# Graph-attention logits in a fused two-layer kernel: first layer through diagonal fp32 matmuls, squares on ScalarE, third layer partly on TensorE, softmax moved into the gather stage

## The reference

```python
sph = jnp.stack([rho, theta, phi], axis=-1)
feat = jnp.concatenate([sph, sph - jnp.mean(sph, axis=-1, keepdims=True)], axis=-1)
h = lrelu(_bn(feat @ W1.T, g1, b1))      # 6 planes
h = lrelu(_bn(h @ W2.T, g2, b2))         # 3 planes
h = lrelu(_bn(h @ W3.T, g3, b3))         # 1 plane
att = jax.nn.softmax(h[..., 0], axis=-1)
agg = jnp.einsum('bnkc,bnk->bnc', xk, att)
return x + agg.transpose(0, 2, 1)
```

## Time and profile before

| | us |
|---|---|
| median of 3 runs | 6926.59 |
| lowest and highest run | 6912.48, 6935.65 |
| the profiled execution: its time, its span | 6927.13, 6925.3 |
| from the start to the logit block | 5136.4 |
| logit block | 526.3 |
| gather stage | 1262.6 |

### The profile page before, as it was taken

One profiled execution on the slowest core, in us unless ns is written; L12 is line 12 of the kernel. 1 busy time (PEld: TensorE's weight loads), 2 busy tenths in 40 slices (PEclk: granted clock), 3 DMA queues, 4 the chain that ended last, 5 costly groups with the idle time before them and its releaser, 6 DMA issues. The chain is left out here.

```text
span 6925.3 us, 166962 instructions
## 1 busy us (share of the span) xinstructions
PE 4994.0 (72%) x63824; PEld 2889.3 (42%) x63824; DVE 5517.1 (80%) x7158; ACT 3973.8 (57%) x8974; POOL 2391.2 (35%) x3108
## 2 busy tenths in 40 slices
PE   6887887878778787878878778884000029999999
PEld 3444444444444444444444444442000017676676
DVE  8877777878778777877877878873779988888887
ACT  4666655666566566665655556665322237777776
POOL 2444444444444444544544444443000001111111
PEclk8878878887887887887887787885555559999999
DMA  1000000000000000000000000000000000000000
GB/s 37 13 14 14 14 14 26 14 14 14 14 14 26 14 14 14 14 14 26 14 14 14 14 14 26 14 7 4 0 0 0 0 7 33 29 30 29 32 29 27
DMA packets 35795, 114.00 MB, mean 16 GB/s; under 512 B 5488, under 2 KB 6128, under 8 KB 34800
## 3 DMA queue, kind: packets, MB, share of 16 engines
q1 hardware_dynamic: 34928, 102.28, 4.2%
HBM read 68.71 MB, written 33.55 MB: 15 GB/s over the span
## 5 line engine op out<-in xcount | busy, mean ns | idle before, releaser
L550 ACT ACTIVATE ohT<-oh_ps,cst 128x512 bf16<-128x512 f32 x1920 | 1277.1, 691 | 388.1 <-PE oh_ps L430 383.3
L448 PE MATMUL g_ps<-tparts,ohT 128*128 128x24 bf16 x23040 | 921.5, 178 | 797.6 <-ACT ohT L550 787.7
L448 PEld LDWEIGHTS g_ps<-tparts,ohT 128*128 128x128 bf16 x23040 | 765.3, 100 | 1438.2 <-ACT ohT L550 1336.0
L794 DVE MAX8 vals<-pd_sb 128x8 f32<-128x1024 f32 x1024 | 1205.3, 1213 | 133.2 <-ACT pd_sb L550 112.5
L799 DVE FIND_INDEX8 idx<-vals,pd_sb 128x8 uint16<-128x1024 f32 x1024 | 1244.2, 1218 | 0.0
L801 DVE MATCH_REPLACE8 pd_sb<-vals,pd_sb 128x1024 f32<-128x1024 f32 x768 | 927.7, 1208 | 0.0
L430 PE MATMUL oh_ps<-bitsT,code 128*128 128x512 bf16 x1920 | 872.7, 460 | 2.2 <-ACT bitsT L707 2.2
L550 ACT ACTIVATE pd_sb<-pd_ps,nxx 128x512 f32<-128x512 f32 x512 | 355.1, 694 | 864.9 <-PE pd_ps L354 864.2
L1684 PEld LDWEIGHTS e_a_ps<-planes,e_oh 120*128 120x128 bf16 x24576 | 688.1, 97 | 244.1 <-issue 179.1
L818 DVE TENSOR_REDUCE mx<-s_ps 128x8 f32<-128x512 f32 x256 | 176.5, 689 | 721.1 <-PE s_ps L389 721.1
L1500 ACT COPY e_at<-e_a_ps 128x512 f32<-128x512 f32 x512 | 546.0, 1066 | 328.5 <-PE e_a_ps L1684 324.2
(11 more groups left out here) (200 smaller groups left out, 7531.6 us busy)
## 6 DMA issues: line engine op xcount, KB each, us to landing
ctx_s<-in_ctx SPq DMA_DIRECT2D x32, 512.0 KB, 4.2
maskb<-in_mask_Bx1x_ff SPq DMA_DIRECT2D x32, 512.0 KB, 5.0
x_s<-in_x SPq DMA_DIRECT2D x32, 512.0 KB, 5.8
y_spill<-y_s SPq DMA_DIRECT2D x32, 512.0 KB, 2.9
e_y<-y_spill SPq DMA_DIRECT2D x32, 512.0 KB, 4.1
out<-e_o SPq DMA_DIRECT2D x64, 256.0 KB, 2.0
pd_sb<-in_shape_constants SPq DMA_DIRECT2D x1, 1024.0 KB, 5.0
cst<-in_shape_constants SPq DMA_DIRECT2D x1, 242.5 KB, 2.6
```

The costliest lines, as they stand in the source:

```text
L448: m = nc.tensor.matmul(g_ps[:, k % GK, t, :], ohT[:, k % 2, bass.ts(t, P)], tparts[:, par, part, :], start=(part == 0), stop=(part == PART ...
L550: return nc.scalar.activation(dst, src, func, scale=scale, bias=bias)
L794: nc.vector.max(vals[:, i, :], pd_sb[:, (t + i) % RING, :]).then_inc(topk_step, 1)
```

## The change

- **Sums.** ACT sums two planes at the end of the first block and DVE the third, at the same time.
- **Covariance.** DVE keeps the three mixed products; ACT makes the three squares in parallel.
- **Layer 1.** DVE writes 18 diagonal matrices of 128 by 128 (`diag`) from the weights. The columns go in 5 chunks of 1536. For each chunk and each of six planes PE makes 3 x 3 fp32 matmuls of 512 columns into one of two PSUM tiles `made_ps`, ACT scales them into a ring of four tiles `h1`, and DVE does the leaky ReLU and the three products. DVE's passes of the two terms and ACT's copies of `h` back into `planes` are gone, and the statistics are taken chunk by chunk.
- **Layer 3.** For each chunk ACT scales three planes and makes a ReLU of plane 2; PE turns both into the third term by two diagonals (`bend3`), and DVE does the other two planes and the sum.
- **Softmax.** The scale of layer 3 is kept in `last_bn`. The whole softmax is done for 240 columns at a time inside the gather stage, two batches ahead, on ACT (`logits`, `exponent`) and DVE (`soft`). The split into parts (`rows`, `digits`) and `norm` move from POOL to DVE. POOL has no work in the stage.

```diff
-                for i in range(3):
+                for i in range(2):
...
+                v.tensor_reduce(small["sum3"][:, 2:3], planes[:, 2, :], AX.X, ALU.add).then_inc(vstep, 1)
...
+                    nc.tensor.matmul(tot_ps[:, bank, at:at + w], ones, src, start=True, stop=True).then_inc(summed, 1)
+
+                def make(n):
+                    c, j = divmod(n, C1)
+                    if n >= 2:
+                        pe.wait_ge(h1_ready, n - 1)
+                    for s in range(SUB):
+                        for i in range(3):
+                            m = nc.tensor.matmul(made_ps[n % 2][:, s, :], diag[:, j, i, :], planes[:, i, bass.ts(c * SUB + s, BN)],
+                                                 start=(i == 0), stop=(i == 2))
+                    m.then_inc(made, 1)
...
+                make(0)
+                make(1)
+                pe.wait_ge(squared, 3)
+                pe.wait_ge(crossed, 3)
+                total(1, S["cov"][:], 6)
+                for n in range(2, NC * C1):
+                    make(n)
...
+                for c in range(NC):
+                    pe.wait_ge(g_ready, c * G_PER + 2)
+                    if c >= 2:
+                        pe.wait_ge(h3_step, (c - 2) * H3_PER + 3)
+                    for s in range(SUB):
+                        nc.tensor.matmul(made_ps[c % 2][:, s, :], bend3[:, 0, :], planes[:, 2, bass.ts(c * SUB + s, BN)], start=True, stop=False)
+                        m = nc.tensor.matmul(made_ps[c % 2][:, s, :], bend3[:, 1, :], h1[:, c % 2, bass.ts(s, BN)], start=False, stop=True)
+                    m.then_inc(bent, 1)
...
+                def move(n):
+                    j = n % C1
+                    act.wait_ge(made, n + 1)
+
+                    if n >= TRING:
+                        act.wait_ge(term, (n - TRING + 1) * (C2 + 1))
+                    a.activation(h1[:, n % TRING, :], made_ps[n % 2][:].rearrange("p s w -> p (s w)"), ACT.Identity,
+                                 scale=S["a1"][:, j:j + 1], bias=S["bb"][:, j:j + 1]).then_inc(h1_ready, 1)
...
+                for n, i in enumerate((0, 1, 2)):
+                    if n:
+                        act.wait_ge(squared, n)
+                    a.activation(sq[:], planes[:, i, :], ACT.Square, bias=S["nmean"][:, i:i + 1],
+                                 accum_out=S["cov"][:, n:n + 1]).then_inc(squared, 1)
...
+                for c in range(NC):
+                    affine(c, 2)
+                    act.wait_ge(g_ready, c * G_PER + 1)
+                    if c >= 2:
+                        act.wait_ge(bent, c - 1)
+                    a.activation(h1[:, c % 2, :], planes[:, 2, cols(c)], ACT.Relu).then_inc(g_ready, 1)
+                    affine(c, 0)
+                    affine(c, 1)
...
+                for j in range(C1):
+                    for i in range(3):
+                        m = v.tensor_scalar(diag[:, j, i, :], con["ident"], S["mat"][:, j, i:i + 1], None, ALU.mult)
+                m.then_inc(diag_ready, 1)
+                for n, factor in enumerate((SLOPE, 1.0 - SLOPE)):
+                    m = v.tensor_scalar(bend3[:, n, :], con["ident"], w3b[:, 2:3], factor, ALU.mult, ALU.mult)
+                m.then_inc(diag_ready, 1)
...
+                dve.wait_ge(mean_ready, 1)
+                pairs = [(0, 0), (1, 1), (2, 2), (0, 1), (0, 2), (1, 2)]
+                for n, (i, k) in enumerate(pairs[3:]):
+                    if n:
+                        dve.wait_ge(crossed, n)
+                    v.scalar_tensor_tensor(junk[:], planes[:, i, :], S["mean"][:, i:i + 1], planes[:, k, :],
+                                           ALU.subtract, ALU.mult, accum_out=S["cov"][:, 3 + n:4 + n]).then_inc(crossed, 1)
...
+                for n in range(NC * C1):
+                    c, j = divmod(n, C1)
+                    src = h1[:, n % TRING, :]
+                    at = n * (C2 + 1)
+                    dve.wait_ge(h1_ready, n + 1)
+                    v.scalar_tensor_tensor(src, src, SLOPE, src, ALU.mult, ALU.max).then_inc(term, 1)
+                    dve.wait_ge(term, at + 1)
+                    for i in range(C2):
+                        wij, acc = w2b[:, i, j:j + 1], h2[:, i, :]
+                        if j == 0:
+                            m = v.tensor_scalar(acc, src, wij, None, ALU.mult)
+                        else:
+                            m = v.scalar_tensor_tensor(acc if j < C1 - 1 else planes[:, i, cols(c)], src, wij, acc, ALU.mult, ALU.add)
+                        m.then_inc(term, 1)
...
-                dve.wait_ge(g_out, C2 + 1)
-                do(v.scalar_tensor_tensor(planes[:, 0, :], planes[:, 0, :], SLOPE, planes[:, 0, :], ALU.mult, ALU.max))
-                m = B * QUADS
-                att = planes[:, 0, :].rearrange("p (m k t) -> p m t k", m=m, t=QT)
-                flat = planes[:, 0, :].rearrange("p (m k t) -> p m k t", m=m, t=QT)
-                do(v.tensor_reduce(mxp[:], att, AX.X, ALU.max))
-                v.tensor_tensor(flat, flat, mxp[:].rearrange("p m (o t) -> p m o t", o=1).to_broadcast([P, m, K, QT]),
-                                ALU.subtract).then_inc(e_in, 1)
-                dve.wait_ge(e_out, 1)
-                do(v.tensor_reduce(smp[:], att, AX.X, ALU.add))
-                do(v.reciprocal(smp[:], smp[:]))
-                do(v.tensor_tensor(flat, flat, smp[:].rearrange("p m (o t) -> p m o t", o=1).to_broadcast([P, m, K, QT]), ALU.mult))
...
+                for c in range(NC):
+                    g0, g1 = planes[:, 0, cols(c)], planes[:, 1, cols(c)]
+                    dve.wait_ge(g_ready, c * G_PER + 3)
+                    v.scalar_tensor_tensor(g0, g0, SLOPE, g0, ALU.mult, ALU.max).then_inc(h3_step, 1)
+                    dve.wait_ge(g_ready, c * G_PER + 4)
+                    v.scalar_tensor_tensor(g1, g1, SLOPE, g1, ALU.mult, ALU.max).then_inc(h3_step, 1)
+                    dve.wait_ge(h3_step, c * H3_PER + 1)
+                    dve.wait_ge(bent, c + 1)
+                    v.scalar_tensor_tensor(g0, g0, w3b[:, 0:1], made_ps[c % 2][:].rearrange("p s w -> p (s w)"), ALU.mult, ALU.add).then_inc(h3_step, 1)
+                    dve.wait_ge(h3_step, c * H3_PER + 3)
+                    v.scalar_tensor_tensor(g0, g1, w3b[:, 1:2], g0, ALU.mult, ALU.add).then_inc(h3_step, 1)
...
+                        if g == 0 and q == QUADS - 1 and further:
+                            logits(b + 2)
+                        if g == 5 and q == QUADS - 1 and further:
+                            exponent(b + 2)
                         if g in (3, 4, 5, 6) and ahead:
...
-            def rows(b):
...
-                v.tensor_copy(rowsb[:, DIGITS, :], whole).then_inc(part_step, 1)
-                gate(pool, part_step, n + 1, e_pool_gates)
-                v.tensor_tensor(rest[:], whole, rowsb[:, DIGITS, :], ALU.subtract).then_inc(part_step, 1)
-                gate(pool, part_step, n + 2, e_pool_gates)
-                v.tensor_copy(rowsb[:, DIGITS + 1, :], rest[:]).then_inc(part_step, 1)
-                pool.wait_ge(part_step, n + 3)
-                v.tensor_tensor(rowsb[:, DIGITS + 2, :], rest[:], rowsb[:, DIGITS + 1, :], ALU.subtract).then_inc(rows_ready, 1)
-                gate(pool, digits_cut, (b + 1) * DIGITS, e_pool_gates)
-                v.tensor_copy(rowsb[:, 0:DIGITS, :], dig16[:]).then_inc(rows_ready, 1)
...
+            def soft(b, step):
+
+                if step == 0:
+                    dve.wait_ge(z_ready, b + 1)
+                    v.scalar_tensor_tensor(z[:], z[:], SLOPE, z[:], ALU.mult, ALU.max).then_inc(z_bent, 1)
+                    dve.wait_ge(z_bent, b + 1)
+                    v.tensor_reduce(peak[:], z[:].rearrange("p (q k t) -> p q t k", q=QUADS, t=QT), AX.X, ALU.max).then_inc(soft_step, 1)
+                elif step == 1:
+                    dve.wait_ge(soft_step, b * SOFT + 1)
+                    v.tensor_tensor(shape4(z[:]), shape4(z[:]), same(peak[:]), ALU.subtract).then_inc(z_low, 1)
+                elif step == 2:
+                    dve.wait_ge(z_exp, b + 1)
+                    v.tensor_reduce(total[:], z[:].rearrange("p (q k t) -> p q t k", q=QUADS, t=QT), AX.X, ALU.add).then_inc(soft_step, 1)
+                elif step == 3:
+                    dve.wait_ge(soft_step, b * SOFT + 2)
+                    v.reciprocal(total[:], total[:]).then_inc(soft_step, 1)
+                else:
+                    dve.wait_ge(soft_step, b * SOFT + 3)
+                    v.tensor_tensor(shape4(att_s[:]), shape4(z[:]), same(total[:]), ALU.mult).then_inc(soft_step, 1)
...
+                    v.tensor_copy(rowsb[:, DIGITS, :], att_s[:]).then_inc(soft_step, 1)
+                elif step == 1:
+                    v.tensor_tensor(rest[:], att_s[:], rowsb[:, DIGITS, :], ALU.subtract).then_inc(soft_step, 1)
+                elif step == 2:
+                    v.tensor_copy(rowsb[:, DIGITS + 1, :], rest[:]).then_inc(soft_step, 1)
+                else:
```

(14 more changed lines are left out.)

331 lines of the change are left out of this document (162 added, 169 removed).

## The result

The changed kernel takes 6772.97 us (median of 4 runs, 6771.79 to 6778.47); the kernel before, over 4 runs, 6931.12. The ratio is 0.9778, with a 95% interval of 0.9759 to 0.9798. The forecast was 6751, with a range of 6717 to 6812. The profiled execution went from 6927.1 to 6771.9 us: 155.2 less, where the sum said 176.2. So some 21 us are missing, and they can be placed.

A forecast was written before the change was run, and what follows sets the result against it. DVE was taken to bound the logit block, PE the gather stage with DVE close behind. The terms summed to -176.2 us, from 6927.1 to 6750.9, so 6751 was forecast, range 6717 to 6812.

The forecast's parts named there:

- Sums, diagonals, covariance, tiny steps: Up to the covariance's end: sums -6.6 us, diagonals +3.2, covariance products shared between DVE and ACT -24.9, tiny steps -1.3.
- Rival D: Covariance: ACT's squares and DVE's products run in turn, winning 4 instead of 25 us, 6772 in all; chance 0.05.
- Layers 1 and 2: Logit block: PE becomes the bound by a hair at 7.87 us a step; 238.4 us against 331.4, -93.0.
- rival C: Layer 1: PE's clock stays at the half or keeps dropping there; 6973 us, 46 slower; chance 0.05.
- Layer 3: Logit block: from the scale to the last statistics 55 us instead of 61.2, so -6.2.
- The prediction's other branch: Layer 3: PE's clock stays at the half, a chunk costs PE 10.4 us and the layer takes 60.7.
- Softmax and head: Softmax block goes but for the barrier, -67.4 us; DVE's new work in the gather stage's head costs +6.
- Gather stage, +14: Gather stage: DVE's new work fits, but PE waits about 0.3 us more at two places; +14 us, bounds -16 and +50.
- Rival A: Gather stage pays 49 us more, 6800: small operations dearer, or the clock falls once in a batch; chance 0.16.
- where the loop jumps back PE stands still anyway: Gather stage: at loop jumps PE stands still over 2 us, covering the first added wait; only 0.3 us counted, 15 times.
- The price of DVE's new work: Gather stage: 4.7 us new on DVE for each batch, some 1.4 given back as POOL's contention goes.
- Rival B: Gather stage wins 16 us instead of losing 14, POOL's contention having made most of PE's waits; 6721; chance 0.10.

The follow-up runs named there:

- x8: The changed kernel with eight matmuls for each plane of a chunk, not nine, and PE's gather loop pinned to slot 226; 6763.17 us in a single run.
- x5: The changed kernel with the scaled softmax and two digit cuts of the next batch behind the second one-hot tile in DVE's queue; 6773.71 us, ratio 0.9788.
- x3: The kernel before, nothing of the change in it, with PE's gather loop pinned to slot 226 of a block; 6949.17 us, ratio 1.0042.
- x7: The changed kernel's new logit block with the softmax over all pairs and the gather stage of the kernel before; 6826.78 us, ratio 0.9862.
- x1: The changed kernel with PE's gather loop pinned to slot 0, the start of a block; 6744.61 us, ratio 0.9745.
- x6: The changed kernel with the softmax's split into three parts and the digits' cast back on POOL; 6779.98 us, ratio 0.9806.
- x10: The kernel before with PE's gather loop pinned to slot 0 of a block; 6926.06 us, ratio 1.0004.

## Why the prediction was right, and where 21 us went

- **Sums, diagonals, covariance, tiny steps:** 6.6 and 22.8 us measured, 6.6 and 23.0 in the sum. Rival D is refuted by the rows above.
- **Layers 1 and 2:** -96.1, not -93.0. A step takes 7.72 us, not 7.87; PE is the bound and DVE hardly less, confirmed by x8. At each of PE's three starts after idle time in the logit block the granted clock was 0.50 for 5.8 to 6.2 us and then 1.00: rival C is refuted. (In the first half batch of the gather stage, where PE waits often for DVE, it was 0.50 for 19 us.) The prediction's price of an fp32 matmul, 0.865 us, comes from the eight of the earlier trace rows in 7.13 us, less the run-out of the last, and its 1.72 at half clock from the two in 3.51; the changed kernel's matmuls took 0.858 at 1.00 and, at the start of layer 3, 1.71 at 0.50. The 2.2 us for a start at half clock were an estimate that no run shows: PE's start in this stretch stood at 0.50 for 5.8 us, by these prices 2.9 us more than at 1.00.
- **Layer 3:** -8.4, not -6.2 with the same tiny steps. PE started at a granted clock of 0.50, was at 1.00 within 7 us, and stayed there through waits of 0.6 and 3.4 us (rows below). The prediction's other branch, 60.7 with the clock at the half, did not come; 52.8 did. That branch was hardly put to the test, since PE had two waits in five chunks and not 3.9 us in each.
- **Softmax and head:** -67.9 as in the sum; the head with the first half batch +3.8, not +6.
- **Gather stage, +14: this is the step that failed.** It was +43.9. The part for ordinary batches was right in the mechanism, 17 x 0.6 = 10 us expected and 10.5 found. But the prediction split it in two halves of 0.3, for the three instructions ahead of the second tile and for the wait on the exponential. The tile's wait grew by 0.54, and the other half didn't come: DVE waits 1.27 us for the exponential, but PE's other wait in the batch stayed at 0.44. Rival A's other branch, the clock falling in a batch, came in 6 of 17 (+8.7), which x5 ties to the length of the wait. And "where the loop jumps back PE stands still anyway" was priced at 0.3 us each, when it cost 2.0. That is 26 us, because the change in another stage moved the loop against the blocks in which PE's program is loaded. x3 shows that alone makes 27 us of stage, x7 that the logit block does it, x1 that 24 to 28 come back by a pin. The order of the queues, which I compared, could not show it; a count of PE's instructions could.
- **The price of DVE's new work:** too high. DVE rose by 2.0 us a batch (32.47 to 34.51) against my 4.7 - 1.4 = 3.3 (the earlier trace rows has the former). PE did not feel it, nor what x6 changed in DVE's work, so the error had no effect that the runs show. Rival B, a gather stage 16 us faster, did not come about: with POOL gone PE's second wait in a batch is 0.44 us as before, and the first is longer.

Two sums of the prediction are a little off: 17 x 0.6 + 15 x 0.3 is 14.7 and not 14, and rival C's 28 steps at the half clock cost 28 x 7.6 = 213 us more and not 216. Neither matters. The rows of layer 3 (PE's first matmuls, the rest, and its longer wait):

```profile
5406.02:5412.59 6.57, 6.57 (x9) 2.72 (x9) 3.43 (x2) 6.54 (x5) 0.00 (x0) 0.53 0.00 0
5412.59:5439.58 26.99, 22.95 (x53) 9.52 (x51) 24.78 (x21) 21.08 (x14) 0.00 (x0) 1.00 0.00 0
5434.19 1.10 PE L1220 MATMUL made_ps<-planes,bend 128*128 128x512 f32 x2 [3.43 <-DVE planes L1382]
```

The forecast was within 22 us because the logit block, which holds most of the sum, was priced from rows of the same instructions. It won 6 us more than said (and 1.4 came from elsewhere), the gather stage 28 us less. Part of this is luck: the range reached up to 6812 for rival A, whose price was for other causes, and the 26 us of the jumps, which nobody had priced, fell inside it. With the loop at position 0 the same change takes 6744.61 us, 6 below the forecast.

## What to carry to other kernels

When a change adds or removes instructions ahead of a hardware loop, count them on each engine: the loop's place in the blocks of 256 can cost or win 2 us for each jump (43.30 us in x3, 41.12 in the kernel before), in a stage that the change doesn't touch, and a pin at the block's start takes the luck out. Without the change such a pin won nothing (x10), as the kernel before stood at a good place by chance. In a queue that runs in strict order, put what the critical engine needs next ahead of every instruction that waits for that engine; here that, with the pin, was worth 84 us (80 by the ratios), half of what the whole change won. And ask of each small operation not what it costs but what stands behind it: of 2.0 us more of DVE's work in a batch PE felt only the 0.65 that stood between the residual sum and the next tile.

## What the runs showed of the hardware that I had not expected

- PE waited 2.2 to 2.8 us at a jump to position 226 of a block and again 1.8 to 4.2 us some 30 instructions on; at position 0 it waited once, 3.3 to 3.9 us. It went on 1.6 to 2.4 us after the end of an instruction transfer at the first wait, and 1.0 to 1.6 us after one at the second.
- A hint that announces the jump changed neither wait (2.34 and 2.40 us).
- With a wait of 1.1 us in each batch of an otherwise full stream of matmuls the granted clock fell in 4 to 9 of 17 ordinary batches; with waits of 0.44 to 0.58 us alone it fell in none of 100 (six kernels, less the two batches in which PE also waited for "issue").
- DVE's products of 128x7680 took 8.22 us beside ACT's squares of the same size, as they had alone; the squares took 6.71 us, between the 6.60 and 6.79 of ACT's other passes of that size.
